# One core of a Trainium2 chip: the inverse x step of a spectral layer as 64x64 tiles in four parts

## The reference

```python
h_ft = jnp.fft.rfft2(h)
out_modes = jnp.einsum('bixy,ioxy->boxy', h_ft[:, :, :16, :16], w_c)
spec = jnp.fft.irfft2(out_modes, s=(64, 64))
h = leaky(spec + conv3x3(h, conv_w[i]) + conv_b[i])
```

## Time and profile before

| | us |
|---|---|
| median of 3 runs | 1229.78 (1228.11 to 1233.86) |
| the profiled execution | 1232.76 |
| its span in the trace | 1231.0 |
| mean granted clock of TensorE | 0.973 |

### The profile page before, as it was taken

One profiled execution on the slowest core, in us unless ns is written; L12 is line 12 of the kernel. 1 busy time (PEld: TensorE's weight loads), 2 busy tenths in 40 slices (PEclk: granted clock), 3 DMA queues, 4 the chain that ended last, 5 costly groups with the idle time before them and its releaser, 6 DMA issues.

```text
span 1231.0 us, 47951 instructions
## 1 busy us (share of the span) xinstructions
PE 1137.8 (92%) x22416; PEld 652.9 (53%) x22416; DVE 531.6 (43%) x548; ACT 481.2 (39%) x887; POOL 84.0 (7%) x154
## 2 busy tenths in 40 slices
PE   3699999899999999899999999988999999899964
PEld 2466666555555555655555556534444454366722
DVE  2655665344445343544445434301221323277843
ACT  1145555223333333223333334223344343466523
POOL 2000000000000000000000000011212020120000
PEclk9899999999999999999999999999999999899986
DMA  9364446386676667777777777396664554000000
GB/s 310 137 214 136 149 142 198 128 278 211 202 211 208 205 214 213 239 220 214 214 214 214 213 213 215 73 209 147 148 141 91 136 127 96 4 6 1 2 1 17
DMA packets 51573, 194.24 MB, mean 158 GB/s; under 512 B 15696, under 2 KB 16464, under 8 KB 41808
## 3 DMA queue, kind: packets, MB, share of 16 engines
q1 hardware_dynamic: 41392, 138.22, 42.3%
q0 software_dynamic: 9984, 52.97, 11.2%
HBM read 138.18 MB, written 52.95 MB: 155 GB/s over the span
## 4 chain that ended last, share of the span: by engine, by line
PE 85%; DVE 5%; issue 3%; ACT 2%; DMA 1%; SPq 1%; ACTq 0%; DVEq 0%
PE psum L637 19%; PE psum L597 14%; PE psum L611 13%; PE psum L624 6%; PE psum L570 5%; PE psum L582 5%; PE psum L515 4%; PE psum L501 4%; PE psum L555 3%; PE psum L651 2%; PE psum L835 2%; DMA halo<-activations 1%; PE psum L659 1%; PE psum L699 1%; DVE vt L1217 1%
## 5 line engine op out<-in xcount | busy, mean ns | idle before, releaser
L1014 ACT ACTIVATE x_now<-psum,conv_bias 128x512 f32<-128x512 f32 x256 | 176.6, 690 | 476.3 <-PE psum L637 459.5
L637 PE MATMUL psum<-dft,vt 128*32 128x128 f32 x8192 | 244.9, 274 | 11.7 <-issue 10.7
L637 PEld LDWEIGHTS psum<-dft,vt 128*32 128x32 f32 x8192 | 222.2, 110 | 51.8 <-issue 50.2
L1194 DVE STREAM_TRANSPOSE ft<-psum 128x1024 f32<-128x1024 f32 x50 | 101.4, 2029 | 280.6 <-PE psum L501 280.6
L1217 DVE STREAM_TRANSPOSE vt<-psum 128x1024 f32<-128x1024 f32 x64 | 126.6, 1978 | 203.1 <-PE psum L570 203.1
L597 PE MATMUL psum<-halo,conv 128*128 128x512 f32 x384 | 180.7, 612 | 1.2 <-DMA halo<-activations 1.2
L611 PE MATMUL psum<-halo,conv 64*32 64x512 f32 x3072 | 176.9, 592 | 0.0
L321 ACT ACTIVATE spec<-psum 32x128 f32<-32x128 f32 x372 | 142.0, 382 | 38.7 <-PE psum L515 34.9
L1187 DVE STREAM_TRANSPOSE xt<-x_now 128x1024 f32<-128x1024 f32 x100 | 123.9, 1242 | 64.9 <-ACT x_now L1014 58.9
L611 PEld LDWEIGHTS psum<-halo,conv 64*32 64x32 f32 x3072 | 53.7, 106 | 114.5 <-issue 114.3
L597 PEld LDWEIGHTS psum<-halo,conv 128*128 128x128 f32 x384 | 69.9, 192 | 83.5 <-issue 72.8
(11 more groups left out here) (149 smaller groups left out, 780.1 us busy)
## 6 DMA issues: line engine op xcount, KB each, us to landing
halo<-activations SPq DMA_DIRECT2D x512, 132.0 KB, 5.2
activations<-x_now POOLq DMA_DIRECT2D x48, 1056.0 KB, 7.1
halo<-activations SPq DMA_DIRECT2D x64, 528.0 KB, 4.2
wspec<-in_spec SPq DMA_DIRECT2D x16, 1024.0 KB, 10.3
xcol<-in_xcol SPq DMA_DIRECT2D x16, 384.0 KB, 4.5
x_now<-in_ser SPq DMA_DIRECT2D x2, 1056.0 KB, 7.3
spec<-in_onehot SPq DMA_DIRECT2D x1, 2048.0 KB, 17.1
wspec<-in_causal SPq DMA_DIRECT2D x1, 2048.0 KB, 27.2
```

The lines of the kernel that those rows point to most:

```text
L637: z = mm(acc[u][g:g + 32, 128 * ih:128 * ih + 128], vt[:, k, 4 * u + ih, r, :], ix[:, s, :], start=False, stop=True, skip_group_check=True)
L1014: copy(x_now[:, k, 16 * u:16 * u + 16, 0:G], acc[u].rearrange("p (i j) -> p i j", j=G), ACT.Prelu, bias=conv_bias[:, l:l + 1], alpha=SLOPE ...
```

## The change

The parities are kept in the order (s, r), with r reversed in units 2 and 3, from layer 0 on; x and y change places in the two transforms, and the constants and weights are laid out for it. `spectral` takes the two row parities of a channel together: a product has 64 rows of `vt` (one row half il) and 64 columns (r, channel) as weights and streams `ix`, 64 columns, to one of two strips of 64 output partitions. The four tiles (il, s) write two units at once. Part 0 and part 2 hold units 0 and 1, with il exchanged, part 1 and 3 units 2 and 3. Parts 2 and 3 wait for parts 0 and 1 (`s_half`), and `s_acc` is raised in them only. `turn_x` takes one image of the pair at a time (every other row of `x_now`, read down its columns) instead of the lower and the upper rows of both, and both wait for all four evictions. `mix` waits for all spectrum copies before its first part. `conv0` is made by three copies instead of one. `load_halo` issues 11 DMAs for every pair. `head_out` comes after part 1.

```diff
-        dft = sb("dft", [128, 704])
+        dft = sb("dft", [128, 544])
-        conv = sb("conv", [128, NL - 1, 448])
+        conv = sb("conv", [128, NL - 1, 512])
-        conv0 = sb("conv0", [96, 128])
+        conv0 = sb("conv0", [96, 2, 128])
...
                 for h in range(2):
-                    if turn(l - 1, h) == 0:
-                        sp.dma_start(halo[:, k, 0, to:to + n], x_d[p, :, of:of + n]).then_inc(s_halo[k], 16)
                     for f in range(4):
-                        if turn(l - 1, h) != 0:
-                            g = 32 * (f ^ turn(l - 1, h))
-                            sp.dma_start(halo[32 * f:32 * f + 32, k, 0, to:to + n],
-                                         x_d[p, g:g + 32, of:of + n]).then_inc(s_halo[k], 16)
-                        g = 32 * ((2 * (f % 2) + f // 2) ^ turn(l - 1, h))
-                        sp.dma_start(halo[32 * f:32 * f + 32, k, 1, to:to + n],
+                        g = 32 * (2 * (f % 2) + (f // 2 ^ h))
+                        sp.dma_start(halo[32 * f:32 * f + 32, k, 0, to:to + n],
                                      x_d[p, g:g + 32, of:of + n]).then_inc(s_halo[k], 16)
+                    if h == 0:
+                        sp.dma_start(halo[:, k, 1, to:to + n], x_d[p, :, of:of + n]).then_inc(s_halo[k], 16)
+                    for f in range(2):
+                        if h == 1:
+                            g = 64 * (1 - f)
+                            sp.dma_start(halo[64 * f:64 * f + 64, k, 1, to:to + n],
+                                         x_d[p, g:g + 64, of:of + n]).then_inc(s_halo[k], 16)
...
-                            z = mm(rowed[g:g + 32, f ^ (turn(l, h) // 2), :],
-                                   ex[64 * f:64 * f + 64, turn(l, h) % 2, :],
-                                   xt[64 * f:64 * f + 64, 32 * h + m:32 * h + 32:2, :], start=True, stop=True)
+                            at = 32 * m + 16 * h
+                            z = mm(rowed[g:g + 32, f, :], ex[64 * f:64 * f + 64, :],
+                                   xt[64 * f:64 * f + 64, at:at + 16, :], start=True, stop=True)
...
                 if l > 0:
                     pe.wait_ge(s_spec_act, l)
-                    pe.wait_ge(s_spec_dve, 2 * l - 1)
+                    pe.wait_ge(s_spec, l * PAIRS + 2)
+                    pe.wait_ge(s_spec_dve, 2 * l)
                 for c in range(4):
-                    if l > 0 and c == 1:
-                        pe.wait_ge(s_spec, l * PAIRS + 2)
-                        pe.wait_ge(s_spec_dve, 2 * l)
...
-            def spectral(T, u):
-                l, p = place(T)
+            def spectral(T, part):
                 k = T % 2
-                pe.wait_ge(s_vt, T + 1)
+                if part == 0:
+                    pe.wait_ge(s_vt, T + 1)
+                if part >= 2:
+                    pe.wait_ge(s_half, 2 * T + part - 1)
                 for ih in range(4):
-                    for r in range(2):
-                        for s in range(2):
-                            g = 32 * ((2 * r + s) ^ turn(l, u // 2))
-                            z = mm(acc[u][g:g + 32, 128 * ih:128 * ih + 128], vt[:, k, 4 * u + ih, r, :],
-                                   ix[:, s, :], start=False, stop=True, skip_group_check=True)
-                z.then_inc(s_acc, 1)
+                    for s in range(2):
+                        for e in range(2):
+                            u, il = 2 * (part % 2) + e, e ^ (part // 2)
+                            at = 128 * ih + 64 * il
+                            z = mm(acc[u][64 * s:64 * s + 64, at:at + 64],
+                                   vt[64 * il:64 * il + 64, k, 4 * u + ih].rearrange("p r o -> p (r o)"),
+                                   ix[64 * il:64 * il + 64, s, :], start=False, stop=True, skip_group_check=True)
+                            if part >= 2 and ih == 3 and s == 1:
+                                z.then_inc(s_acc, 1)
+                if part < 2:
+                    z.then_inc(s_half, 1)
...
-                for u in range(4):
-                    spectral(T, u)
-                    if p > 0 and u == 0:
+                for part in range(4):
+                    spectral(T, part)
+                    if p > 0 and part == 1:
                         head_out(p - 1)
...
-            copy(conv0[:], spare[0:96, 0:128], ACT.Identity).then_inc(s_conv0, 1)
+            folded = spare[0:96, 0:128].rearrange("p (s r o) -> p s r o", s=2, r=2)
+            copy(conv0[:, 0, :], spare[0:96, 0:128], ACT.Identity)
+            for r in range(2):
+                z = copy(conv0[:, 1, :].rearrange("p (s r o) -> p s r o", s=2, r=2)[:, :, r, :], folded[:, :, 1 - r, :],
+                         ACT.Identity)
+            z.then_inc(s_conv0, 1)
...
-            def turn_x(n, h):
+            def turn_x(n, m):
                 if n < 2:
                     dve.wait_ge(s_ser[n], 16)
                 else:
-                    dve.wait_ge(s_x, 4 * (n - 2) + 2 * h + 2)
+                    dve.wait_ge(s_x, 4 * (n - 2) + 4)
                 reached(dve, s_fx, n)
-                vec.transpose(xt[:, 32 * h:32 * h + 32, :],
-                              x_now[:, n % 2, 32 * h:32 * h + 32, 0:G]).then_inc(s_xt, 1)
+                vec.transpose(xt[:, 32 * m:32 * m + 32, :],
+                              x_now[:, n % 2, :, 0:G].rearrange("p (i m) j -> p m j i", m=2)[:, m]).then_inc(s_xt, 1)
```

More of the change, by code:

```diff
@@ new lines, in dft_constants @@
+    for c in range(4):
+        for fb in range(2):
+            for half in range(2):
+                k2 = 4 * c + 2 * fb + half
+                w = (1.0 if k2 == 0 else 2.0) / (H * W)
+                for s in range(2):
+                    a = th * k2 * (2 * g + s)
+                    for b in range(2):
+                        ix[:, fb, half, 0, c, b, s, b] = w * np.cos(a)
+                        ix[:, fb, half, 1, c, b, s, b] = -w * np.sin(a)
+    parts = [ex.reshape(128, 32), ey.reshape(128, 128), iy.reshape(128, 256), ix.reshape(128, 128)]
```

129 lines of the change are left out of this document (59 added, 70 removed).

## The result

The changed kernel takes 1216.84 us (median of 10 runs, 1206.24 to 1223.97) against 1228.94 for the kernel before (10 runs on the same chip): a ratio of 0.9897, 95% interval 0.9864 to 0.993. That is faster by 12 us, where 50 were forecast, and outside the range of 1154 to 1210. The profiled execution took 1218.4 (span 1216.6).

A forecast was written before the change was run, and what follows sets the result against it. TensorE, busy 92% of the span, was taken as the bound. Layer 0 9.7, layers 1 and 2 26, boundaries 0 and layer 3 14.5 summed to 50 us off: 1180 us, range 1154 to 1210.

The forecast's parts named there:

- The products: Inverse x step: 128 products a pair at 15.0 ns, 1.92 us in place of 3.63, 1.71 us less.
- serial loads in a shared strip: Inverse x step: row halves sharing a strip don't load weights side by side, step 3.84 us, whole 1265; chance 0.10.
- drained parts: Inverse x step: waits between parts drain the array, 0.5 us each, two a pair; whole about 1215; chance 0.07.
- the floor of 25 ns a start: Inverse x step: fixed cost of 25 ns a product, step 3.2 us, whole 1233; chance 0.03.
- The transposes: Both turns of x wait for all four evictions and take 1.25 us each, with 1.98 as the other end.
- this rival: Dear transposes: turns of 1.98 us, layer 0 period 10.5 us, whole 1194; chance 0.08.
- Layer 0: ScalarE takes over the bound: period about 9.7 us, 0.54 gained a pair, 9.7 us off in all.
- a sign of being wrong: TensorE's granted clock, 0.97 over the whole before, falling in the new gaps of layer 0.
- Layers 1 and 2: Evictions, turns and copies are hidden, late code takes part of the saving: 0.86 us a pair, 26 us for 30 pairs.
- I estimate 1.25 us of pauses a pair: Layers 1 and 2: late instruction packets, 0.85 us a pair more than before; ends 0 and 1.71 more.
- The boundaries: Mode mixing waits +0.75 us, first forward x step +0.45, pauses 0.5: these eat the 1.71, zero for all three.
- Layer 3: Centre waits for x_now; 3 us off in five plain pairs, 13 in ten, 1.5 less halo stall: 14.5 in all.

The follow-up runs named there:

- the run that reads in order: The changed kernel with both turns of x reading x_now in memory order (wrong values, same amount): 1211.75 us, ratio 0.9865.
- all orders changed: The changed kernel with cb and cf apart in layers 1 and 2, layer 0 reordered, cb behind the step in layer 3: 1189.5 us, ratio 0.9702.
- the last runs: Two kernels with split rows products (packet's end at two places), halo's second copy loaded for the first two pairs only: 1188.7 and 1209.85 us.
- the split kernel: The changed kernel with 19 of 32 rows products a pair in layers 1 and 2 made as two of 256 columns: 1253.78 us, ratio 1.0192.

## Why the prediction was wrong

**The products: right.** 15.8 ns against 15.0 (the earlier trace rows was the right row to take), the clean pair 13.97 us against a forecast 13.7: the step takes 2.02 for 1.92, and cf 1.03 for 0.89. The rivals of serial loads in a shared strip and of drained parts are out; so is the floor of 25 ns a start, which the Trainium skill ("TensorE: Matmul & The Clock Gate", section "Wait — 56ns, not 53.3ns?") states: 128 products in 2.02 us lie closer than that.

**The transposes: wrong, at the first of two readings.** I took 1.25 us from the strided read of PSUM and kept 1.98 as the other end. It is 2.08, beyond that end. The row nearest by operation was not nearest by memory. The period of 10.5 us that I gave for this rival is what layer 0 has, 10.56.

**Layer 0: wrong by 17 us** (+7.5 for -9.7). The turn is 4.2 us of it, by the run that reads in order. Pauses at a packet's end, which I put at nothing there, are in that run's ring too, and they are 12.5 us in layer 0 after the change against 6.0 before. The order was the larger matter: the ring of step, evictions, turns, forward x and inverse y was named by me link by link, but as given. With the step ahead of rf and cb, and cf among the convolution, the layer takes 181.4 us. (4.38 + 3.15 is 7.53, not 7.55; nothing hangs on it.) Its granted clock, which I had named as a sign of being wrong, did fall: 0.96 in place of 1.00 over the loop of layer 0 (46 to 190 us), and 1.00 again with all orders changed.

**Layers 1 and 2: the mechanism right, the size wrong, and this is the largest term**: 2 us for 26. The failed step is "I estimate 1.25 us of pauses a pair". Three things were mis-sized. The clean pair gives 1.45 us and not 1.71, 43.5 us for 30 pairs. Pauses without a releaser went from 8.4 to 36.6 us, 0.94 more a pair and not 0.85; the twelve pairs above lie on average 1.61 us over the clean one, those of before 0.44, which is 1.2 more. And a term stood at nothing, the clock. TensorE's busy time in the two layers fell from 514.7 to 480.8 us, 34 of the 43.5, while the granted clock fell from 1.00 to 0.98 and 0.99: by my estimate that is up to 8 us (0.02 x 265 + 0.01 x 261). It falls behind long pauses. In the second pair of layer 1 it was 0.71 over the centre products:

```profile
260.52 2.95 issue
...
264.17 5.16 PE psum L593 x8
```

They take 5.16 us there and 3.64 in the clean pair. Idle time rose from 13.0 to 44.8 us, 34 less 32 is the 2 that were gained.

The estimate of the pauses counted how many instructions a dense run has and nothing of what a packet must share its way with. Two numbers would have been needed. In the changed kernel the 256 instructions that end in such a pause take 2.6 to 3.9 us where the packet moves within 1.2 us of their start. Where it is held up beside the halo's loads they take up to 7.0. The earlier trace rows showed a pause of the second kind: its 256 instructions start at 422.11, and the DMA view of 422.11 to 425.2 was not read.

```profile
q1 hardware_dynamic: 226, 0.64, 88.3%
```

The packet moves at 425.31, and TensorE goes on at 427.94.

**The boundaries** can't be read apart from this; they lie within the sums of the layers. Their term has a number without a row: by the earlier trace rows, in layer 0, the second turn of before ends 149.71 + 1.25 - 145.29 = 5.67 us after the step's start, not 6.45, so the first forward x step was to come 1.2 us later and not 0.45.

**Layer 3: right and a little better**, 19.1 us for 14.5. The chain of a pair there shows each link of the forecast: step, head's output behind part 1, a wait for x_now, centre.

```profile
856.84 1.09 PE psum L636 x64
857.93 0.99 PE psum L662 x8
858.93 0.70 PE psum L636 x32
859.62 0.68 ACT x_now L1017
...
860.35 1.13 PE psum L593 x2
```

The pair takes 865.37 - 849.28 = 16.09 us against 16.71. This layer has few pauses at packets' ends in either kernel: the heads' and fronts' products stretch the packets. The stall for the halo is 17.52 us, not shorter.

**Left open.** How the remaining difference of layer 0 (3.3 us with turns in order) divides into pauses and the clock wasn't tried apart. How much of the time in layers 1 and 2 is the clock's is an estimate. A later start of the halo's loads, which the last runs suggest, wasn't tried.

## What to carry to other kernels

Count instructions as well as columns. When products get short, take TensorE's stream in stretches of 256 instructions and ask of each how long it lasts: here those of up to 3.9 us could stall, and beside large transfers those of up to 7 us. Such a stall shows as "issue" without a releaser, in gaps that lie a multiple of 256 instructions apart. It shrank here with long products between the short ones and with fewer transfers, and not by making the short ones shorter; behind long stalls the granted clock was lower, too. And look at what a new order puts side by side: the one that parted the short products brought waits for evictions. And before a step is made to wait for all units of a pair, write down the ring through the other engines and try its order on paper.

## What the runs showed of the hardware

- Four 64x64 tiles, with weight loads of 64 columns in both row halves, take a float32 product each 15.8 ns (2.02 us for 128, the changed kernel).
- VectorE's transpose of 128x1024 float32 from SBUF takes 1.22 to 1.24 us in order and 2.04 to 2.08 read down columns, though it writes in order; the strided read of PSUM takes 1.25.
- A semaphore increment on TensorE's queue cost 65 ns that matmuls didn't hide ((18.90 - 13.97)/76); a product of 512 columns split in two cost 25 ns ((14.44 - 13.97)/19).
- After the pause of 2.32 us in the split kernel, the granted clock was 0.76 over the next 7.15 us, where it had been 1.00.
- A packet's transfer is short, 1.2 us at the pause of 2.32 us, but its instructions run only 2.7 us after it starts (376.42 to 379.15); 2.2 to 3.0 us over the 40 pauses of the changed kernel.
- With the halo's queue filling 96.2% of the DMA engines (372.83 to 376.35) the packet started 3.6 us after the 256 instructions ahead of it; with the engines nearly idle the 256 instructions up to a pause took 3.3 us (398.31 to 401.59).
